# A graph layer in three passes on one Trainium2 core: edge extraction in nine chunks, eight of them beside layer 0, and four small steps moved to GpSimd

## The reference

```python
def sage(h, w_self, w_neigh, b):
    agg = segment_sum(h[src], dst, num_segments=n) * inv_deg
    return h @ w_self + agg @ w_neigh + b
h = maximum(layernorm(x), 0.0)
h = relu(sage(h, ws0, wn0, b0))      # 128 -> 256
h = relu(sage(h, ws1, wn1, b1))      # 256 -> 256
h = sage(h, ws2, wn2, b2)            # 256 -> 128
out = x + h
```

## Time and profile before

| | us |
|---|---|
| median of 3 runs | 4386.35 |
| lowest, highest | 4383.37, 4386.78 |
| the profiled execution | 4345.58 |
| its span, first to last instruction | 4343.4 |

### The profile page before, as it was taken

One profiled execution on the slowest core, in us unless ns is written; L12 is line 12 of the kernel. 1 busy time (PEld: TensorE's weight loads), 2 busy tenths in 40 slices (PEclk: granted clock), 3 DMA queues, 4 the chain that ended last, 5 costly groups with the idle time before them and its releaser, 6 DMA issues. The chain is left out here.

```text
span 4343.4 us, 111247 instructions
## 1 busy us (share of the span) xinstructions
PE 3606.9 (83%) x22511; PEld 3214.4 (74%) x22511; DVE 3539.2 (81%) x12507; ACT 3039.1 (70%) x8013; POOL 2257.1 (52%) x2513
## 2 busy tenths in 40 slices
PE   0799999999999999999878888887878766666665
PEld 0688888888888888888777777777777755555555
DVE  8899999999999999999767676666766756666666
ACT  1688888888888888888666666666666656666666
POOL 0444444444444444444355555555555556666665
PEclk9999999999999999999999999999999965555556
DMA  1244444444444444444466666666666677777777
GB/s 50 86 143 142 140 141 143 142 140 141 144 141 139 142 143 140 139 142 143 135 177 193 191 193 194 192 194 189 195 195 194 192 199 219 217 223 218 214 221 207
DMA packets 1040774, 727.06 MB, mean 167 GB/s; under 512 B 103208, under 2 KB 1012656, under 8 KB 1040632
## 3 DMA queue, kind: packets, MB, share of 16 engines
q1 hardware_dynamic: 854298, 569.93, 44.0%
q0 software_dynamic: 80848, 104.93, 10.1%
q10 hardware_dynamic: 105600, 51.92, 4.0%
HBM read 451.60 MB, written 360.71 MB: 187 GB/s over the span
## 5 line engine op out<-in xcount | busy, mean ns | idle before, releaser
L587 POOL DMA_INDIRECT loaded_rows<-in_x,gather_at x784 | 858.4, 1095 | 1048.5 <-ACT h_nbr L694 906.9
L1276 PE MATMUL ps_out<-w_hi,hid_hi 128*128 128x512 f32 (+1 forms) x3136 | 1113.7, 355 | 253.1 <-DVE hid_lo L1169 96.9
L601 POOL DMA_INDIRECT layer_mem<-p_rows,gather_at x784 | 784.8, 1001 | 586.7 <-issue 223.1
L1276 PE MATMUL ps_out<-w_hi,hid_lo 128*128 128x512 f32 (+1 forms) x3136 | 1072.2, 342 | 0.0
L1276 PE MATMUL ps_out<-w_lo,hid_hi 128*128 128x512 f32 (+1 forms) x3136 | 1067.8, 341 | 0.0
L1276 PEld LDWEIGHTS ps_out<-w_hi,hid_hi 128*128 128x128 f32 x3136 | 595.9, 190 | 405.2 <-issue 242.8
L614 POOL DMA_INDIRECT layer_mem<-z_rows,gather_at x528 | 525.8, 996 | 322.3 <-issue 153.2
L1276 PEld LDWEIGHTS ps_out<-w_hi,hid_lo 128*128 128x128 f32 x3136 | 595.3, 190 | 72.8
L1276 PEld LDWEIGHTS ps_out<-w_lo,hid_hi 128*128 128x128 f32 x3136 | 597.8, 191 | 58.4
L1169 DVE SCALAR_TENSOR_TENSOR hid_lo<-ps_out,hid_hi 128x512 fp32r<-128x512 f32 x392 | 270.2, 689 | 400.1 <-ACT hid_hi L777 330.6
L788 ACT ACTIVATE layer_mem<-iota_row,triple_node 128x128 f32<-128x128 f32 x1056 | 347.5, 391 | 259.5 <-issue 178.8
(11 more groups left out here) (163 smaller groups left out, 8933.1 us busy)
## 6 DMA issues: line engine op xcount, KB each, us to landing
p_rows<-stored_rows SPq DMA_DIRECT2D x392, 256.0 KB, 2.2
q_rows<-layer_mem SPq DMA_DIRECT2D x392, 256.0 KB, 2.6
loaded_rows<-q_rows SPq DMA_DIRECT2D x392, 256.0 KB
loaded_rows<-y_rows SPq DMA_DIRECT2D x264, 192.0 KB
layer_mem<-in_x SPq DMA_DIRECT2D x264, 192.0 KB
out_rows<-stored_rows ACTq DMA_DIRECT2D x264, 192.0 KB
loaded_rows<-in_x SPq DMA_DIRECT2D x392, 128.0 KB
z_rows<-layer_mem SPq DMA_DIRECT2D x392, 128.0 KB
```

The lines of the kernel that those rows point to most:

```text
L587: pool.indirect_dma_start(raw[s.slot][0:rows, 2 + j, :], None, table, bass.IndirectOffsetOnAxis(gather_at[s.slot][0:rows, j:j + 1], axis=0 ...
L601: pool.indirect_dma_start(rows_in[s.slot][0:SLOT_ROWS, j, 0:width], None, table, bass.IndirectOffsetOnAxis(gather_at[s.slot][0:SLOT_ROWS, ...
L1276: ins = nc.tensor.matmul(o, a, b, start=n == 0, stop=n == len(terms) - 1)
```

## The change

- The tiles go in 9 chunks of 88 (before: 7 of 114), and there are 14 rounds instead of 13. In the prologue only chunk 0 is extracted.
- The flag is made from the counts of edges per tile (`edge_count`, summed by ACT), inside the rounds of chunk 0, before the keys are out.
- Layer 0 goes chunk by chunk (44 pairs each). While chunk k runs, DVE extracts chunk k+1: over the first 28 pairs one round per two pairs, `find` (maximum) behind one step and `take` (copy of the 8 keys and match-and-replace) ahead of the next. Then PE transposes the keys of chunk k+1 into a free strip of the bank of the sums, and DVE makes the tables of the chunk. The last chunk's 44 pairs carry the tables of layer 2 instead.
- POOL waits for `tables_made` at each chunk. It now also makes, per pair, a copy of two node columns (`node_now`), `minus_mean`, `shift`, `self_scale` and the one-hots (`node_select`, two tensor-scalar comparisons). A gather now stands behind the `shift` and the one-hots of the pair two before it on POOL's queue.
- DVE and ACT do their parts in another order and with shorter lags (DVE's last is 6 steps back instead of 8, PE's 5 instead of 7, ACT's 4 instead of 5). On ACT the normalisation goes last in a step.

The diff, cut to its core:

```diff
-CHUNKS = 7
-ACT_CHUNKS = 4
+CHUNKS = 9
+ACT_CHUNKS = 5
-ROUNDS = 13
+ROUNDS = 14
+CHUNK_USES = TP // (2 * SLOTS)
+ROUND_USES = ROUNDS // 2
...
+        def run_uses(eng, step, first, last, peel):
+            split = min(max(first, peel), last)
+            peeled(step, first * SLOTS, split * SLOTS, PAIRS)
+            if split < last:
+                looped(eng, step, split, last, PAIRS)
...
             def layer0_gathers(table, rows, by_chunk):
...
+                    t, u = first.back(2), first.back(3)
+                    if t.live():
+                        if t.has(2):
+                            pool.wait_ge(L0.summed, t.back(2).n + 1)
+                        pool.tensor_tensor(node_now[t.half][:, :], slot_node[:, bass.ds(t.n * 2, 2)], ones[:, 0:2],
+                                           ALU.mult).then_inc(L0.node_copied, 1)
+                        pool.wait_ge(L0.moments_ready, t.n + 1)
+                        pool.tensor_tensor(minus_mean[t.half][:, :], moments[t.half][:, :, 0], minus_ones[:, :], ALU.mult
+                                           ).then_inc(L0.mean_turned, 1)
+                        pool.wait_ge(L0.mean_turned, t.n + 1)
+                        pool.wait_ge(L0.rstd_ready, t.n + 1)
+                        if t.has(2):
+                            pool.wait_ge(L0.normed, t.back(2).n + 1)
+                        pool.tensor_tensor(shift[t.half][:, :], minus_mean[t.half][:, :], rstd[t.half][:, :], ALU.mult
+                                           ).then_inc(L0.shift_ready, 1)
+                    if u.live():
+                        two = bass.ds(u.n * 2, 2)
+                        pool.wait_ge(L0.recip_done, u.n + 1)
+                        if t.live():
+                            pool.wait_ge(L0.node_copied, t.n + 1)
+                        pool.tensor_tensor(self_scale[:, two], inv_degree[:, two], fast[:, :].to_broadcast([P, 2]),
+                                           ALU.mult).then_inc(L0.scale_ready, 1)
...
+                    if t.live():
+                        for j in range(2):
+                            last = pool.tensor_scalar(node_select[t.half][:, j, :], iota_row[:, :],
+                                                      node_now[t.half][:, j:j + 1], None, op0=ALU.is_equal)
+                        last.then_inc(L0.selected, 1)
...
+                for c in range(CHUNKS):
+                    pool.wait_ge(tables_made, c + 1)
+                    run_uses(pool, step, *chunk_uses(c), 2)
+                peeled(step, PAIRS, PAIRS + 3, PAIRS)
...
+            for r in range(ROUNDS):
+                best = keys[:, 0, r * 8:(r + 1) * 8]
+                if r:
+                    dve.wait_ge(keys_taken, r)
+                dve.max(best, wf_key[:, 0, :]).then_inc(keys_ready, 1)
+                dve.wait_ge(keys_ready, r + 1)
+                dve.match_replace(wf_key[:, 0, :], best, wf_key[:, 0, :], 0.0).then_inc(keys_taken, 1)
+                if r == 7:
+                    dve.wait_ge(edges_counted, CHUNKS)
+                    dve.tensor_scalar(over[:, 0:CHUNKS], edge_count[:, :], 8.0 * ROUNDS - 0.5, None, op0=ALU.is_gt)
...
+                if r == 10:
+                    dve.wait_ge(faults_summed, 1)
...
+                    dve.sem_inc(flag_set, 1)
...
+                def find():
+                    dve.max(best_now[h][:, :], wf_key[:, c, :]).then_inc(keys_ready, 1)
+
+                def take(use):
+                    n = count(use)
+                    dve.wait_ge(keys_ready, n + (ROUNDS * c + 1))
+                    dve.tensor_copy(keys[:, c, bass.ds(n * 8, 8)], best_now[h][:, :]).then_inc(keys_put, 1)
+                    dve.match_replace(wf_key[:, c, :], best_now[h][:, :], wf_key[:, c, :], 0.0).then_inc(keys_taken, 1)
...
+            def layer0_by_chunk():
...
+                    def step(s):
+                        find, take, taken = halves[s.slot // 2]
+                        if s.slot % 2:
+                            take(s.use)
+                        elif s.slot:
+                            halves[0][2](s.use)
+                        elif s.looped or s.use > first or c > 1:
+                            halves[1][2](s.use - 1)
+                        layer0(s)
+                        if s.slot % 2 == 0:
+                            find()
+                    run_uses(dve, step, first, first + ROUND_USES, 3)
+                    at = (first + ROUND_USES) * SLOTS
+                    if c >= SHARED_CHUNK:
+                        shared_columns(c)
+                    peeled(layer0, at, at + 1, PAIRS)
+                    peeled(lambda s: layer0(s, lambda: read_strips(c)), at + 1, at + 2, PAIRS)
+                    chunk_tables(c)
...
+            def turn_chunk(c):
...
+                last = nc.tensor.matmul(strips[0], keys[:, c, :], ident[0:TP, 0:TP], is_transpose=True,
+                                        start=True, stop=True)
...
```

More of the change, by code:

```diff
@@ L681, in step @@
                 def step(first):
-                    t = first.back(2)
-                    if t.live():
-                        act.wait_ge(L0.shift_ready, t.n + 1)
-                        if t.has(2):
-                            act.wait_ge(L0.summed, t.back(2).n + 1)
-                            act.wait_ge(L0.turned, t.back(2).n + 1)
-                        for j in range(4):
-                            rows = h_own[t.half][:, j, :] if j < 2 else h_nbr[t.half][:, j - 2, 0:D]
-                            if general and j >= 2:
-                                last = act.activation(rows, raw[t.slot][:, j, :], ACT.Copy)
-                            else:
-                                last = act.activation(rows, raw[t.slot][:, j, :], ACT.Relu,
-                                                      bias=shift[t.half][:, j:j + 1], scale=rstd[t.half][:, j:j + 1])
-                        last.then_inc(L0.normed, 1)
                     t = first.back(3)
@@ L732, in step @@
                                        ).then_inc(L0.h1_hi_ready, 1)
+                    t = first.back(1)
+                    if t.live():
+                        act.wait_ge(L0.shift_ready, t.n + 1)
+                        if t.has(2):
+                            act.wait_ge(L0.summed, t.back(2).n + 1)
+                            act.wait_ge(L0.turned, t.back(2).n + 1)
+                        for j in range(4):
+                            rows = h_own[t.half][:, j, :] if j < 2 else h_nbr[t.half][:, j - 2, 0:D]
+                            if general and j >= 2:
+                                last = act.activation(rows, raw[t.slot][:, j, :], ACT.Copy)
+                            else:
+                                last = act.activation(rows, raw[t.slot][:, j, :], ACT.Relu,
+                                                      bias=shift[t.half][:, j:j + 1], scale=rstd[t.half][:, j:j + 1])
+                        last.then_inc(L0.normed, 1)
                 return step
@@ new lines, in layer0 @@
+                if u.live():
+                    dve.wait_ge(L0.std_ready, u.n + 1)
+                    if u.has(2):
+                        dve.wait_ge(L0.normed, u.back(2).n + 1)
+                    dve.reciprocal(rstd[u.half][:, :], std[u.half][:, :]).then_inc(L0.rstd_ready, 1)
+                if t.live():
+                    dve.wait_ge(L0.p_ready, t.n + 1)
+                    dve.wait_ge(L0.scale_ready, t.n + 1)
+                    for j in range(2):
+                        last = dve.scalar_tensor_tensor(q_out[t.slot][:, j, :], p_out[t.slot][:, j, :],
+                                                        self_scale[:, bass.ds(t.n * 2 + j, 1)],
+                                                        ps_out[t.half][:, j * 2 * H + H:(j + 1) * 2 * H],
+                                                        op0=ALU.mult, op1=ALU.add)
+                    last.then_inc(L0.rows_ready, 1)
@@ L1156, in _ @@
+            with dve.If(dve.value_load(general_flag[0:1, 0:1], min_val=0, max_val=1) != 0):
+                pipeline(dve, layer0, PAIRS, 6, rounds=3)
+            with dve.Else():
+                layer0_by_chunk()
             general(1)
```

409 lines of the change are left out of this document (236 added, 173 removed).

## The result

The changed kernel takes **4422.02 us** in the median of 4 runs (4417.48 to 4423.35), the kernel before beside it 4385.35 us (4383.37 to 4386.78): a ratio of **1.0083 [1.0071, 1.0095]**, 37 us slower, where 43 us faster was predicted. The profiled execution took 4421.28 us around its span of 4419.5 us.

The account below looks back on a forecast made before the run. PE, without a gap at 5.107 us a pair, was taken as the bound, DVE 98.7% busy beside it. From 4386.35 us, -53 + 0 + 7 + 2 + 2 = -42 gave 4344, stated as 4343 us, range 4326 to 4378.

Parts of the forecast that it names:

- part 1: Prologue: with only one chunk extracted there, POOL's first copy for layer 0 comes 53 us earlier (48 to 56).
- Part 2: Start and end of layer 0: no change, 0 us, between -8 and +5.
- Part 4: DVE's step in layer 0: 4.6 us without a round, 4.98 and 5.15 with; rounds cost +7 us in all.
- the ring: Layer 0's way round through DVE and ACT, `cat_lo` waiting for `cat_hi`: 4.66 us without a round, 5.04 and 5.21 with.
- The first rival: Layer 0: DVE and ACT bound the rounds, 0.15 us a pair over PE, 34 us in place of 7, 4370 us; chance 0.16.
- The fourth: Rival: the start gains too, two early steps saved (8 us) and no loss in the rounds (7 us), 4328 us; chance 0.08.
- the fifth: Rival: rounds wait for the layer and stand bare, 112 of 1.10 us give 123 us, 4459 us; chance 0.02.
- Part 3: POOL's step in layer 0: 2.7 us plus 1.2 of new work is 3.9 us, at most 6.1, of 5.107.
- the third rival: POOL becomes layer 0's bound if its new work takes over 2.4 us: step 5.5 us, 157 us more, 4500 us; chance 0.09.
- The second rival: Shared port of POOL and DVE: `hid_lo` 0.3 us later in each pair, 67 us on top of 7, 4410 us; chance 0.07.
- Part 5: Layer 0's added small transposes on PE, +2 us (0 to 5.6), and DVE's table steps, +2 us (0 to 10).

Follow-up runs that it names:

- e1: The changed kernel with all nine chunks extracted ahead of layer 0, which runs as one plain loop: ratio 1.0211 to the kernel before, layer 0 2032.9 us.
- e4: The changed kernel with `take` behind the odd step instead of ahead of it: ratio 0.9988 to the kernel before, layer 0 2046.9 us.
- e13: The changed kernel with all chunks extracted ahead of layer 0 and, on ScalarE, `h1` ahead of the square root: ratio 1.0215, layer 0 2034.4 us.
- e12: The kernel of e13 with the one-hots back on VectorE: ratio 1.014 to the kernel before, layer 0 2004.2 us.
- the first, fourth and fifth set: Three of five groups of runs, each beside its own runs of the kernel before, whose median was 4352, 4353 and 4350 us in them.
- e16: e6 run again (changed kernel, `take` behind the odd step, `h1` ahead of the square root, one-hots on VectorE): ratio 0.9932, layer 0 2023.7 us.
- b2: The changed kernel itself run again, in the fourth set: ratio 1.0096 to the kernel before, layer 0 2088.9 us.
- e2: The changed kernel with the one-hots back on VectorE, in one operation behind the statistics: ratio 1.0087 to the kernel before, layer 0 2092.8 us.
- b1: The changed kernel itself run again, in the second set: ratio 1.0063 to the kernel before, layer 0 2077.4 us.
- e6: The kernel of e5 with the one-hots back on VectorE: ratio 0.9887 to the kernel before, layer 0 2009.6 us.
- e11: The kernel of e6 run again, in the third set: ratio 0.9939 to the kernel before, layer 0 2028.4 us.
- e5: The changed kernel with `take` behind the odd step and, on ScalarE, `h1` ahead of the square root: ratio 0.9905, layer 0 2013.7 us.

## Why the prediction was wrong

**The prologue (part 1) was right in kind**, and 5 us too careful: 74.6 us predicted, 69.85 measured, -58 in place of -53. Most of the difference is the windows' landing. It was put 3 us later, and the first wide operation starts at 31.34 us where it started at 31.57: one more count and two more gathers cost nothing there. So the rounds begin at 52.77 us, not 56.5. A round of the bare chain takes 53.83 - 52.77 = 1.06 us, not 1.10. Part 2 said 0 for start and end (-8 to +5); the drain gave 5.4 us, within its bounds.

**Part 4 is the step that failed**, +7 us in place of most of +97: taking the rounds out of the layer (e1) gave 56 us by itself. Part 4 had the ring and its waits, but:
- "A pair of steps with a round adds the maximum to one and copy and replace to the other". The diff has `find` behind the even step and `take` ahead of the odd one; on the engine these are neighbours. The terms were 0.38 and about 0.55 in two steps; measured 1.16 in one. Putting them where the prediction had them (e4) gives 42 us back.
- It took the mean of two steps, 5.125 us, against PE's 5.107. With the round as measured that mean would be 4.66 + 1.16/2 = 5.24 us, and 5.39 was measured. In the rows above the step without a round is 4.76 us (4.66 predicted) and the one with it 5.82: PE stands idle in the long step and doesn't get all of it back in the short one. The 0.15 us between 5.24 and 5.39 is what a mean leaves out, with what GpSimd adds in it; the two weren't tried apart.
- Once in four pairs `p` waits 0.33 us behind the statistics, a wait that the change put ahead of `p`, predicted at 0.1 us. No run took it away.
- "Steps without a round lose nothing (4.66)" was argued from VectorE alone. They lose 0.09 us in e1, of which 0.08 are GpSimd's (e13 to e12).

**The first rival** (DVE and ACT bound the rounds, 4370 us) was nearest: it is this same ring, priced at 0.15 us a pair over PE. Measured are 5.39 - 5.107 = 0.28 us, and 56 us by e1 where it had 34. The fourth had the gain of the drain, and not the rounds without loss; the fifth didn't happen, since rounds ran beside the layer.

**Part 3, and the third rival, were right in kind and wrong in size, on both sides.** The step was put at 3.9 us, at most 6.1, and the point from which it binds at 2.4 us of new work. Measured are two one-hots of 0.64 (predicted 0.23 each, with 0.41 as the upper bound for one), four small operations of 0.20 (0.19), the copy at 0.48 (0.19), in sum 2.1 + 0.46 + 0.48 + 0.81 + 1.28 = 5.13 us (4.98 where the overlap of neighbouring records is left out). The iota was the nearest row by shape, but it reads nothing; the row that reads a tile was the one for the bound, and DVE's price is no bound for GpSimd. The Trainium skill, GPSIMD Engine Reference, section "Elementwise — side-by-side cycle accounting", gives 1.8 cycles per element at best and 2.6 with two inputs at 1.2 GHz, by which 128 elements would take 0.19 to 0.28 us, an estimate, beside the cost of dispatch. The rows of this case don't agree: with the 0.20 us of a small operation taken as the fixed cost they give (0.638 - 0.20)/128 = 3.4 ns per element, some 4 of these cycles, again an estimate. The rival priced at 4500 us was too high: the one-hots on GpSimd cost some 0.08 us in a pair without rounds (5.20 us in e13, 5.13 in e12) and not 0.4, which is 30 us. Part of these 30 can be the shared port, which the one-hots on GpSimd also load.

**The second rival, the shared port,** was right that the two engines meet, and wrong about which one waits. The prediction counted nothing since GpSimd's new work would be nearly over when `hid_lo` starts; but from 300 to 2050 us of the changed kernel 322 of 327 `hid_lo` start while a one-hot is running, with 0.31 us of it left in the mean. Even so `hid_lo` takes 698 ns in the change (1000 to 1500 us) and 682 in e12: VectorE loses next to nothing. GpSimd waits for it: a copy from 1050.32 to 1050.91 us ends behind the `hid_lo` of 1050.18 to 1050.86 us. The rows:

```profile
1050.18 0.68 DVE L1257 TENSOR_TENSOR hid_lo<-layer_mem,hid_hi 128x512 fp32r<-128x512 f32 x1
```

```profile
1049.16 1.20 POOL L644 TENSOR_SCALAR node_select<-iota_row,node_now 128x128 f32<-128x128 f32 x2
1050.32 0.59 POOL L604 COPY gather_at<-slot_index 128x2 int32 x1
```

In e12, whose GpSimd has no one-hots, the copy takes 189 ns in the mean. By the Trainium skill, SBUF — State Buffer, section "SBUF: two separate sides", whoever starts first holds the shared pair and the other blocks for a whole instruction. The rows agree where `hid_lo` starts first: from 300 to 2050 us 263 of these copies start inside a `hid_lo`, and 258 of them end behind it, by 0.045 us in the median. They don't where a one-hot starts first: the `hid_lo` of 1050.18 us starts 0.18 us before the one-hots end and takes its usual 0.68 us. So the loser is GpSimd, which then had no room for it.

**Part 5** had PE's transposes and tables at 4 us, which no run took apart, and nothing for PE's new order. PE's step without a gap is 5.13 us in the change (the sums' products start at 1212.43 and 1217.56 us) against 5.107:

```profile
1212.43 0.61 PE L1469 MATMUL ps_agg<-h_nbr,node_select 128*128 128x130 f32 x4
...
1213.20 0.27 PE L1480 MATMUL ps_turn<-ident,layer_mem 128*128 128x128 f32 x1
1213.23 0.48 PE L1442 MATMUL ps_out<-w_hi,hid_hi 128*128 128x512 f32 x1
1213.55 0.39 PE L1442 MATMUL ps_out<-w_lo,hid_hi 128*128 128x512 f32 x1
...
1217.56 0.61 PE L1469 MATMUL ps_agg<-h_nbr,node_select 128*128 128x130 f32 x4
```

The first 512-column product behind the turns takes 0.32 us to the next where the others take 0.23. Before, a 256-column product stood there:

```profile
1212.16 0.36 PE L1276 MATMUL ps_hid<-cat_hi,w_hi 128*128 128x256 f32 x1
1212.36 0.28 PE L1276 MATMUL ps_hid<-cat_lo,w_hi 128*128 128x256 f32 x1
1212.48 0.28 PE L1276 MATMUL ps_hid<-cat_hi,w_lo 128*128 128x256 f32 x1
```

It took 0.20 us where the next took 0.12, so this excess explains only some 0.01 of the 0.02 us; the rest stays open, and that the order is the cause was not tried by itself. In all it is 0.02 x 391 = 8 us, which no edit gave back.

**The account of the 97 us**, from the first, fourth and fifth set: change to e16 65 us (rounds spread, ScalarE's order, one-hots back), e16 to e12 19.5 us (what the rounds and tables still cost in the layer), e12 to the kernel before 15 us (8 of PE's longer step; and the first 28 pairs ran at 4.84 us before and at 5.06 in e12, which is 6 us). The sum is 99.7, b2's loss. e16, e12 and the kernel before come from different sets, so the last two steps hold within the 3 to 7 us by which sets differ.

## What to carry over

Before work is hidden in the gaps of a pipelined loop, write down the engine's order across the step's border: "behind the even step" and "ahead of the odd step" are the same gap. Weigh the longest step against the bound and not only the mean, since a full engine gets back only a part of what a long step took. An engine that stood at 47% has room only for operations whose price was seen on that engine with that kind of input; take it off again alone, since here removing it first (e2) showed nothing and removing it last showed 30 us.

## What the runs showed of the hardware

Between sets of runs the same kernel can differ by more outside the changed layer than any edit in it. The kernel before took 3930 us in one set and 4350 to 4387 in the others. For the changed kernel, a stretch of layer 1 in b1, and the same stretch in the first profile:

```profile
2250.00:3250.00 1000.00, 967.26 (x7419) 906.40 (x7417) 884.27 (x2594) 793.76 (x2223) 752.24 (x732) 1.00 0.83 243
```

```profile
2250.00:3250.00 1000.00, 797.12 (x5758) 723.78 (x5756) 682.47 (x2014) 624.13 (x1726) 578.90 (x576) 0.97 0.66 189
```

It moved 243 GB/s against 189 with the same code; in layer 0, at 136 and 135 GB/s from 1000 to 1500 us, the two are within 9 us. Even in layer 0 one kernel (e6, e16, e11) took 2009.6, 2023.7 and 2028.4 us. In e11 much of the longer time is in one step of four, 5.51 us in the mean in place of 5.23 in e6: there `h1` starts late, as in this row of ScalarE, though PE's products for it ended 0.85 us earlier.

```profile
614.37 0.84 ACT L750 ACTIVATE layer_mem<-ps_hid,b_col 128x256 f32<-128x256 f32 x2 [1.28 <-PE ps_hid L1438]
```

The looped step is four pairs long, so something in each turn of the loop is a candidate; no run tested it, and it stays open. So does why e5 took 2013.7 us in one set and 2041.0 in another.
